# Reordering two stretches of a hand-written event plan in a one-core attention and mixture-of-experts kernel

## The reference, cut to what matters

```python
mod = (silu(c) @ wmod).reshape(4, 6, 1, -1)       # sa, ca, ga, sb, cb, gb per batch
h = layernorm(x) * (1 + ca) + sa
x = x + ga * attention(h)                         # 16 heads of 128, causal
h = layernorm(x) * (1 + cb) + sb
x = x + gb * ffn(h)

def ffn(x):
    h = x @ down_w + down_b                       # 256 -> 128
    logits = x @ router_w + router_b - 1e-7 * cost
    topv, topi = top_k(softmax(logits), 2)
    gate = softmax(topv)
    out = 0
    for k in range(2):
        for e in range(8):                        # hidden 128, 256, 384, 512, 128, 256, 384, 512
            hm = h * onehot(topi[k])[e]
            acc += gelu(gelu(hm) @ w1[e] + b1[e]) @ w2[e] + b2[e]
        out += acc * gate[k]
    out += 0.1 * (gelu(gelu(h) @ shared_w1 + shared_b1) @ shared_w2 + shared_b2)
    return (out @ up_w + up_b) + (gelu(x) @ core_w + core_b)
```

## Time and profile before

| what | value |
|---|---|
| median of 3 executions | 812.05 us (811.22 to 814.85) |
| the profiled execution | 812.05 us, its span on the core 810.0 us |
| PE busy | 784.7 us, 97% of the span |
| DVE busy | 679.5 us, 84% |
| ACT busy | 628.4 us, 78% |
| POOL busy | 441.2 us, 54% |
| granted TensorE clock, mean | 0.996 |

### The profile page before, as it was taken

How to read it: one execution, slowest core, us unless ns; L and a number is a source line. 1 busy time by engine, 2 the same in 40 slices (tenths; PEclk the granted TensorE clock), 3 DMA queues, 4 the chain that set the end, 5 groups by cost and what they waited for, 6 DMA issues and landing times.

```text
span 810.0 us, 14461 instructions
## 1 busy us (share of the span) xinstructions
PE 784.7 (97%) x4806; PEld 700.6 (86%) x4806; DVE 679.5 (84%) x1649; ACT 628.4 (78%) x1417; POOL 441.2 (54%) x305
## 2 busy tenths in 40 slices
PE   7899899999999999999999999999999989989997
PEld 6789898999999999999999999999999767778786
DVE  4789998888888888888888888889898989887967
ACT  3787878877887788877778888877778968876974
POOL 2555365654456655445566544576545474577654
PEclk9999999999999999999999999999999999999999
DMA  7262233343222444322344332244332230111231
GB/s 264 64 171 68 63 90 93 91 104 86 66 66 66 101 108 108 83 66 66 72 104 106 91 92 66 66 97 115 94 76 60 64 105 34 67 58 66 69 102 53
DMA packets 47593, 70.54 MB, mean 87 GB/s; under 512 B 5536, under 2 KB 38464, under 8 KB 47392
## 3 DMA queue, kind: packets, MB, share of 16 engines
q1 hardware_dynamic: 47008, 68.81, 32.4%
q0 software_dynamic: 368, 0.81, 0.3%
q10 hardware_dynamic: 144, 0.00, 0.0%
HBM read 25.49 MB, written 2.17 MB: 34 GB/s over the span
## 4 chain that ended last, share of the span: by engine, by line
PE 64%; ACT 17%; DVE 11%; issue 5%; POOL 2%; DMA 1%; SPq 0%; DVEq 0%; POOLq 0%
PE M L732 10%; PE M L733 9%; PE M L731 9%; PE T L731 7%; PE T L733 7%; PE T L732 7%; PE S L731 5%; PE S L733 5%; PE S L732 5%; ACT PB L623 4%; ACT PB L672 3%; ACT pth L699 2%; DVE S L1135 2%; ACT qk L685 2%; ACT hh L665 1%
## 5 line engine op out<-in xcount | busy, mean ns | idle before, releaser
L623 ACT ACTIVATE PB<-S,nb 128x128 f32<-128x128 f32 (+3 forms) x256 | 133.9, 533 | 109.9 <-DVE nb L1135 109.9
L580 POOL TENSOR_TENSOR ptl<-ptl,pth 128x640 fp32r<-128x640 f32 x126 | 196.8, 1584 | 31.9 <-ACT pth L699 31.9
L573 POOL TENSOR_TENSOR X<-X,fb 128x512 f32<-128x512 f32 x64 | 83.1, 1299 | 239.5 <-DVE fb L1172 239.5
L672 ACT ACTIVATE PB<-PB,ri 128x256 f32<-128x256 f32 (+3 forms) x256 | 124.5, 580 | 6.4 <-DVE ri L1144 6.3
L1135 DVE CUSTOM_DVE_ANT_0 S<-S,cc 128x128 f32<-128x128 f32 (+3 forms) x256 | 117.6, 523 | 1.3 <-PE S L733 1.3
L1124 DVE TENSOR_TENSOR qk<-M,qk 128x512 fp32r<-128x512 f32 x108 | 74.6, 691 | 45.0 <-ACT qk L685 45.0
L1151 DVE STREAM_TRANSPOSE gab<-PB 128x256 f32<-128x256 f32 (+2 forms) x192 | 109.4, 623 | 0.0
L731 PE MATMUL S<-qk 128*128 128x128 f32 (+3 forms) x256 | 86.6, 338 | 4.6 <-DVE qk L1124 4.6
L699 ACT CAST pth<-ptl 128x640 fp32r<-128x640 f32 x128 | 87.8, 745 | 1.1 <-DMA ptl<-gab 1.1
L731 PE MATMUL M<-hh,W 128*128 128x512 f32 x222 | 86.7, 390 | 0.5 <-DVE hl L1110 0.5
L732 PE MATMUL M<-hl,W 128*128 128x512 f32 x222 | 86.5, 390 | 0.0
(11 more groups left out here) (255 smaller groups left out, 2410.7 us busy)
## 6 DMA issues: line engine op xcount, KB each, us to landing
ptl<-gab SPq DMA_DIRECT2D x256, 160.0 KB, 3.0
stage<-in_wat SPq DMA_DIRECT2D x16, 512.0 KB, 5.0
gab<-scw SPq DMA_DIRECT2D x16, 256.0 KB, 3.2
tmp<-scw SPq DMA_DIRECT2D x16, 256.0 KB, 3.6
X<-in_x SPq DMA_DIRECT2D x3, 512.0 KB, 8.3
stage<-in_wfa SPq DMA_DIRECT2D x3, 512.0 KB, 4.5
out<-X SPq DMA_DIRECT2D x3, 512.0 KB, 2.7
X<-in_wmod SPq DMA_DIRECT2D x1, 1024.0 KB, 11.8
```

Of the source, the lines that this page charges most:

```text
L573: pool.tensor_tensor(X[:, a:a + 512], X[:, a:a + 512], fb[:, c2 * 512:c2 * 512 + 512], ALU.add).then_inc(s_y, 1)
L580: pool.tensor_tensor(ptl[u % 2][:, s], ptl[u % 2][:, s].bitcast(F32), pth[u % 2][:, s].bitcast(F32), ALU.subtract).then_inc(s_pl, 1)
L623: ins = act.activation(PB[:, P_OFF[i]:P_OFF[i] + w], PS[bk][:, a:a + w], ACT.Exp, bias=nb[:, i:i + 1], scale=-1.0, accum_out=sm[:, i:i + 1])
L672: act.activation(p, p, ACT.Copy, scale=ri[:, i:i + 1]).then_inc(s_P3, 1)
```

## The change

Nothing is computed differently and no instruction is added or removed; only places in `ffn_plan()` change.

- `wo` of the last pair but one, second half, goes from slot 0.2 (ahead of `wh 21`) to slot 0.4 (ahead of `wh 22`).
- `wt 0` and the first three `wl` go from slot 0.6 to 0.5.
- Router 1 is now put in ahead of the other events of its slots. Its `rs 3` to `rs 14` go from slots 0.11 to 0.16 to slots 0.9 to 0.15.
- `h2 3` goes from slots 1.1 and 1.4 to 1.0 and 1.3, `D 0` from 1.5 to 1.4; `hs 0`, `gx 0`, `o 0`, `up 0`, `hs 1` and `gx 1` go one slot earlier (the second half of `up 0` two).
- Router 2 starts one slot earlier, its `rs 3` two (1.14 to 1.12), its `rs 14` one (1.18 to 1.17), `wt 2` goes from slot 2.0 to 1.20.

By the bank rule, `wt 0` still takes the bank of that `wo`, `z` of the last head still the one of `r 1`; `D 0`, which took the bank of `D 1`, now takes that of `h2 3, 1`, and `r 2`, which took that of `h2 3, 1`, takes that of `D 1`.

```diff
     put(0, 1, ("wo", last - 1, 0), ("rs", 0, 13), ("rs", 0, 14))
-    put(0, 2, ("wo", last - 1, 1), ("wh", 21))
+    put(0, 2, ("wh", 21))
     put(0, 3, ("pt", NU - 1))
-    put(0, 4, ("wx", last - 1, 1), ("wh", 22))
-    put(0, 6, ("wt", 0), ("wl", 0), ("wl", 1), ("wl", 2), ("d0", 0))
+    put(0, 4, ("wo", last - 1, 1), ("wh", 22))
+    router(1, ((0, 5), (0, 6), (0, (9, 9, 9, 11, 11, 12, 12, 14, 14, 14, 15, 15))), (0, 19))
+    put(0, 5, ("wt", 0), ("wl", 0), ("wl", 1), ("wl", 2))
+    put(0, 6, ("d0", 0))
     put(0, 7, ("z", NU - 1), ("st", 6, 0), ("st", 6, 1), ("d0", 1))
     put(0, 8, ("wo", last, 0), ("st", 6, 2), ("st", 6, 3), ("d0", 2))
     put(0, 9, ("wo", last, 1), ("wl", 3), ("nb", 6))
...
-    router(1, ((0, 5), (0, 6), (0, (11, 11, 11, 12, 12, 14, 14, 15, 15, 15, 16, 16))), (0, 19))
-    put(1, 1, ("h2", 3, 0))
-    put(1, 3, ("D", 1))
-    put(1, 4, ("h2", 3, 1))
-    put(1, 5, ("D", 0), ("hs", 0, 0))
-    put(1, 7, ("gx", 0, 0), ("hs", 0, 1))
-    put(1, 9, ("gx", 0, 1))
-    router(2, ((1, 6), (1, 8), (1, (14, 14, 14, 15, 15, 16, 16, 17, 17, 17, 18, 18))), (2, 0))
+    put(1, 0, ("h2", 3, 0))
+    put(1, 3, ("h2", 3, 1))
+    put(1, 4, ("D", 0), ("hs", 0, 0))
+    put(1, 6, ("gx", 0, 0), ("hs", 0, 1))
+    put(1, 8, ("gx", 0, 1))
+    router(2, ((1, 5), (1, 7), (1, (12, 12, 12, 14, 14, 15, 15, 16, 16, 16, 17, 17))), (1, 20))
     router(3, ((2, 4), (2, 5), (2, (11, 11, 11, 12, 12, 14, 14, 15, 15, 15, 16, 16))), (2, 19))
     for t in range(1, B):
         first = t == 1
         put(t, 0, ("xb", t - 1))
-        if not first:
-            put(t, 3, ("D", t))
-        put(t, 7 if first else 6, ("o", t - 1))
-        put(t, 12 if first else 8, ("up", t - 1, 0))
-        put(t, 14 if first else 9, ("up", t - 1, 1))
-        put(t, 11 if first else 9, ("hs", t, 0))
-        put(t, 15 if first else 11, ("gx", t, 0), ("hs", t, 1))
-        put(t, 18 if first else 14, ("gx", t, 1))
+        put(t, 3, ("D", t))
+        put(t, 6, ("o", t - 1))
+        put(t, 11 if first else 8, ("up", t - 1, 0))
+        put(t, 12 if first else 9, ("up", t - 1, 1))
+        put(t, 10 if first else 9, ("hs", t, 0))
+        put(t, 14 if first else 11, ("gx", t, 0), ("hs", t, 1))
+        put(t, 17 if first else 14, ("gx", t, 1))
```

## The result

The changed kernel is slower. In the first comparison five executions took 818.77 to 822.13 us, median 820.78, against 812.05 for the kernel before; the ratio is 1.0093, with a 95% interval of 1.0067 to 1.0118. The forecast of 815.8 had the sign and missed the size: the range ended at 819.5. A second comparison, with 29 executions of the kernel before (median 813.39) and 6 of the changed one (819.49), gave 1.0074, interval 1.0050 to 1.0099, so 6.0 us. The profiled execution after took 817.69 us with a span of 815.6, 5.6 over the one before.

What follows compares the result with a forecast made beforehand. PE, busy 97% of the span, was taken as the bound, so only its gaps between 640 and 726 us count. 3.7 + 0.7 + 1.4 - 2.07 = +3.7 us on 812.05 gave 815.8; own range 814.2 to 817.5, wider range 811.8 to 819.5.

Steps and rivals of the forecast that it cites:

- Step A: Moved `wo` and `wt 0`: PE waits 3.5 us ahead of `wt 0`, half clock follows, last head's chain 2.2 us late.
- Step B: Router 1's `rs 3` in slot 0.9: DVE stands 2.0 us for the fourth power; +3.7 us, +0.7 for the clock.
- Step C: Tile 1 with `h2 3` and `D 0` earlier: gap ahead of `D 0` grows from 0.23 to 2.2; +1.4 us.
- Step D: Router 2 earlier: the wait of 2.07 us ahead of tile 2's first `w1` vanishes; -2.07 us.
- Rival 1: Whole kernel: the same waits but no extra half clock; +1.8 us, 813.9 us; chance 0.23.
- rival 2: Moved waits find their condition met, fourth power done before DVE reaches `rs 3`; -3.9 to -5.6, 807.3 us; chance 0.07.
- rival 4: Whole kernel: no effect, new waits only replace old ones and the last gap stays; 812 us; chance 0.10.
- Rival 3: More half clocks: ahead of `h2 2,0`, `D 0` and at `r 2`, fifth power partly late; +7.2, 819.3 us; chance 0.15.

Runs made afterwards that it cites:

- rs3_late: Changed kernel with `rs 3` to `rs 5` of router 1 one slot later (0.10): 816.69 us, ratio 1.0036 to the kernel before.
- undo_router1: Changed kernel with `rs 3` to `rs 14` of router 1 back in slots 0.11 to 0.16: 818.73 us, ratio 1.0039 to the kernel before.
- tile1_only: Kernel before with the edits of tile 1 alone (router 2 and `wt 2` included): 816.32 us against 815.04, ratio 1.0025.
- after_dn2: Changed kernel with `dn 2` heading slot 1.17, router 2's `rs 10` to `rs 14` behind it, `wt 2` in 2.1: 817.75 us, ratio 1.0041 to the kernel before.
- after_filled: Changed kernel with 40 matmuls of zeros on PE in the gap ahead of `wt 0`: 817.46 us, ratio 1.0044 to the kernel before.
- part 1: The edits of `wo` and `wt 0`; alone on the kernel before: 818.46 us against 814.14, ratio 1.0049.
- undo_tile1: Changed kernel with all of tile 1, router 2 and `wt 2` as before: 819.8 us against 815.04, ratio 1.0052 to the kernel before.
- part 3: The edits of tile 1, with router 2 and `wt 2`; alone on the kernel before: 816.32 us against 815.04, ratio 1.0025.
- d0_late: Changed kernel with `D 0` alone back in slot 1.5: 819.49 us against 814.45, ratio 1.0068 to the kernel before.
- dn2_first: Kernel before with `rs 10` to `rs 14` of router 2 in slots 1.18 and 1.19, `wt 2` in 2.1: 812.07 us against 814.45, ratio 0.9978.

## Why the prediction was right in sign and wrong in size

- **Step A (+2.2 us): right in kind; its errors mostly cancelled.** On the numbers of the step, `z` was to start some 2.7 us later (652.5 less 651.54, and 1.7 for the clock), and its low part 2.2 later (0.6 and 1.7 make 2.3). Measured from the start of tile 0, `z` starts at 18.44 instead of 16.25, +2.19, and its low part 1.6 later. The new gap is 2.45 us, not 3.5: DVE's split of 1024 columns took 1.21 us instead of the 2.17 of the earlier trace rows. The half clock lasted 6.8 us, not 3.4; its first 2 us fell on an idle PE.
- **Step B (+3.7, and +0.7 for the clock): the mechanism right, the sum in part by luck.** DVE's stand was forecast at 2.0 us and is 1.99. `nb 6` was forecast 4.75 late (3.5 and 1.25) and is 4.2, and `h2 2,0` starts 3.1 late, not 3.7; the half clock behind it then cost 1.5 us where I had counted 0.7. At `dta 0` PE was 4.7 us late, 4.4 forecast. `rs3_late` and `undo_router1` show the cause.
- **Step C (+1.4): near in time, but its content was half wrong.** The gap ahead of `D 0` was forecast at 2.2 and is 1.18. I had overlooked that `h2 3,0` takes the bank of `wt 1`, whose reading stands in DVE's queue (1.14 us), and had put it among the edits that cost nothing. The 0.87 ahead of `up 0` I had not seen either. Together the gaps of tile 1 grew by 3.0 us. By router 2 the lateness had grown by 1.8; behind it the half clock of the earlier trace rows, which I had taken to come in both kernels, did not come in this one, and ahead of tile 2 PE was 6.0 late, 1.3 more than at `dta 0`. That this is near 1.4 is luck.
- **Step D (-2.07): failed.** It had the wait ahead of tile 2 vanish; the gaps there are 2.12 us together, so nothing is gained. This is 2.1 of the 2.3 us by which the profiled execution, counted from the start of tile 0, went over the forecast (+6.0 against +3.7). The fifth power ended at 727.0 where I had 724.6: the first power did start ahead of `acc`, but at 706.56, and from there to the end of the fifth it was 20.4 us and not 18.6. DVE read `dn 2` at 731.20, not by 728.5, because all of `rs 10` to `rs 14` stand between the power and this read; before, `rs 13` and `rs 14` stood behind it, and the read came 1.7 us behind the power's step. And `wt 2`, moved from behind tile 2's first `w1` to ahead of it, waits for the router's last step. Before, `w1` alone waited; now both do, one behind the other. I had counted this move at nothing, because PE comes later. `tile1_only` shows the miss alone, `after_dn2` shows that the two places are the cause. The 2.07 itself was no firm number: without the half clock of the earlier trace rows the old order waits 3.05 to 3.09.
- With step D at 0 the forecast would have been 817.9, and the profiled execution took 817.69. This agreement is partly luck, by the cancelling in steps A to C and because it was the shortest of the eight executions on record. The median lies 3.1 us higher. The start of tile 0, where nothing changes, and the number of stretches at half clock both vary from one execution to the next by as much; which of them made this difference is not shown.
- Two readings of the prediction were off besides. "All gaps and the clock" are not under 7 us: the four gaps named are 5.2, but all gaps behind the start of tile 0 are 6.3, and with the clock 8.0. And the narrow matmuls of router 2 had no small gaps; in PE's listing they start 0.11 us apart without idle time.
- **The rivals.** Rival 1 (no half clock) is refuted by the clock rows, and `after_filled` gives its price; rival 2 by DVE's stand at 663.6, rival 4 by the interval. Rival 3 is nearest in time, partly for its reason: the half clock behind `h2 2,0` came in full, and the one behind `wt 0` was twice as long as I took it. But its sum held step D's -2.07 as well, and its stretches behind `D 0` and router 2 did not come.

## What to carry to other kernels

In a plan that all engines walk in order, an event moved one slot earlier is a wait moved ahead of whatever followed it: for each, ask what it waits for on every engine, down to the bank it takes, and what ready work it now stands in front of. A gap that "a later PE will cover" has to be priced like the others, since the late PE meets engines that are late for the same reason. A wait can cost more than its length: at `wt 0`, directly behind narrow matmuls, the half clock added some 2.4 us to a wait of 2.45. And a gap read from one trace is only as firm as that trace: the 2.07 ahead of tile 2 was 3.05 wherever PE had not been slowed before it.

## What the runs showed of the hardware that was not expected

DVE's split of weights (line 1055) and POOL's low part of the last head (line 579) begin within 0.4 us of each other in the kernels with part 1, and who is first goes with how long DVE's split takes. DVE first, in the kernel after: 1.21 us. POOL first, in `undo_tile1`, by the same order of work: 2.46 us, and the gap ahead of `wt 0` is 3.67 instead of 2.45. DVE was first in nine of the ten traces that have `wo` behind the split, and its split took 1.21 or 1.22 us in all nine. In the seven other traces POOL was first by 0.4 to 0.6 us, and the split took 1.97 to 2.23. These are DVE and then POOL of the kernel after, and the same two of `undo_tile1`:

```profile
644.15 1.21 DVE L1055 TENSOR_TENSOR W<-stage,W 128x1024 fp32r<-128x1024 f32 x1
```

```profile
644.34 3.93 POOL L579 TENSOR_TENSOR ptl<-ptl,pth 128x640 fp32r<-128x640 f32 x2 [1.21 <-ACT pth L698]
```

```profile
643.59 2.46 DVE L1057 TENSOR_TENSOR W<-stage,W 128x1024 fp32r<-128x1024 f32 x1
```

```profile
643.43 4.02 POOL L581 TENSOR_TENSOR ptl<-ptl,pth 128x640 fp32r<-128x640 f32 x2 [0.86 <-ACT pth L700]
```

The same kernel's traces also differ in when the clock is at half: the kernel after had 10.2 us of it behind the start of tile 0 in one execution and 13.7 in the other, with equal gaps. One more stretch is 1.7 us, nearly as much as part 3 of this change, so a single profile cannot rank such edits. Over the 17 traces, half clock followed

- the 2.42 to 3.67 us of waiting behind router 1's narrow matmuls in all 8 traces that have it (6.8 us in seven, 3.4 in `d0_late`);
- the 2.53 to 2.74 us ahead of `h2 2,0` in 8 of 9, and the 1.0 us there in none of 8;
- the 3.05 to 3.09 us ahead of tile 2 in all 3;
- the 1.86 to 1.88 us ahead of `z`, behind full-width products, in 1 of 7 (`dn2_first`).

Behind router 2's narrow matmuls alone, with no wait, it came in 2 of 17.
